# Sums of squares over four slots instead of two, a ring of 18 hidden tiles, and eight hidden units moved from GpSimd to ScalarE

## What is computed

```python
hi = x @ W1[:H];  hj = x @ W1[H:]
h = relu(hi[:, :, None, :] + hj[:, None, :, :] + b1)    # 128 x 128 pairs of nodes
y = h @ W2 + b2
y = layernorm(y) * gamma + beta                         # over the features of each pair
out = sum over j of adj[i, j] * y[i, j]
x = layernorm(x + out)
```

## Time and profile before

| what | value |
|---|---|
| median of 3 runs | 2771.56 us (2769.07 to 2772.95) |
| profiled execution | 2773.57 us, span of its instructions 2772.0 us |
| PE busy | 98% |
| PE weight loads busy | 41% |
| DVE busy | 94% |
| ACT busy | 93% |
| POOL busy | 90% |
| granted TensorE clock | 0.989 mean |

### The profile page before, as it was taken

The page is one execution under the profiler, slowest core; times in us unless marked ns, Lnnn a source line. Parts: engine busy times, 40 slices in busy tenths (PEclk is TensorE's granted clock), DMA queues, the critical chain, the costliest instruction groups (busy, mean ns, idle before and its releaser), DMA issues.

```text
span 2772.0 us, 60903 instructions
## 1 busy us (share of the span) xinstructions
PE 2707.0 (98%) x10882; PEld 1128.4 (41%) x10882; DVE 2618.7 (94%) x20102; ACT 2565.2 (93%) x6903; POOL 2491.0 (90%) x3498
## 2 busy tenths in 40 slices
PE   8999999999999999999999999999999999999993
PEld 2344444444444444444444444444444444444442
DVE  4999999999999999999999999999999999999997
ACT  7999999999999999999999999999999999999991
POOL 3899999999999999999999999999999989999992
PEclk9999999999999999999999999999999999999995
DMA  3655655655555555556556555555555565465552
GB/s 104 239 195 211 234 198 197 230 215 192 214 226 202 204 216 222 195 213 234 195 198 235 209 192 227 223 193 210 226 207 195 205 234 203 192 228 222 193 214 108
DMA packets 188668, 571.72 MB, mean 206 GB/s; under 512 B 70656, under 2 KB 106368, under 8 KB 139136
## 3 DMA queue, kind: packets, MB, share of 16 engines
q1 hardware_dynamic: 188288, 567.83, 54.5%
HBM read 555.17 MB, written 8.39 MB: 203 GB/s over the span
## 4 chain that ended last, share of the span: by engine, by line
PE 59%; DVE 13%; ACT 11%; DMA 10%; issue 5%; SPq 2%; POOL 0%; DVEq 0%; POOLq 0%; ACTq 0%
PE y_ps L416 41%; PE ss_ps L428 11%; DVE h L684 8%; ACT h L555 6%; DMA cb<-c_scratch 6%; ACT sq L565 3%; DMA c_scratch<-c 2%; DMA devs<-dev_rows 2%; SPq L324 1%; ACT dev_rows L572 1%; PE prod_bank L478 1%; PE prod_bank L482 1%; DVE h L668 1%; DVE stats L708 1%; DVE gT L684 1%
## 5 line engine op out<-in xcount | busy, mean ns | idle before, releaser
L923 POOL TENSOR_SCALAR h<-vT,uT 128x128 f32<-128x128 f32 x2520 | 2063.8, 834 | 54.1 <-ACT vT L545 44.6
L684 DVE CUSTOM_DVE_ANT_0 h<-h,cb 128x128 f32<-128x128 f32 x8192 | 2005.8, 291 | 74.4 <-DMA cb<-c_scratch 71.4
L416 PE MATMUL y_ps<-h,w2c 128*128 128x512 f32 x4096 | 2032.8, 613 | 11.9 <-DVE h L668 2.8
L555 ACT ACTIVATE h<-uv_ps,uT 128x128 f32<-128x128 f32 x4785 | 1426.9, 441 | 0.0
L565 ACT ACTIVATE sq<-y_ps,b2c_col 128x1024 f32<-128x1024 f32 x1024 | 1193.5, 1166 | 139.3 <-PE y_ps L416 138.6
L416 PEld LDWEIGHTS y_ps<-h,w2c 128*128 128x128 f32 x4096 | 672.9, 190 | 944.1 <-issue 647.3
L684 DVE DVE_READ_ACCUMULATOR2_ANT gT<- 128x1 f32 x8192 | 637.5, 78 | 0.0
L428 PE MATMUL ss_ps<-sq,sel 128*32 128x512 f32 x4096 | 545.5, 605 | 0.8 <-ACT sq L565 0.8
L914 POOL TENSOR_TENSOR rs<-var_eps,minus_half 128x1 f32<-128x1 f32 x448 | 297.9, 665 | 35.1
L911 POOL TENSOR_TENSOR var_eps<-mv,eps_col 128x1 f32<-128x1 f32 x448 | 94.8, 212 | 132.7 <-DVE mv L711 129.2
L668 DVE TENSOR_SCALAR h<-vT,uT 128x128 f32<-128x128 f32 x757 | 202.1, 295 | 4.7 <-ACT mask_all L610 2.6
(11 more groups left out here) (100 smaller groups left out, 1460.6 us busy)
## 6 DMA issues: line engine op xcount, KB each, us to landing
cb<-c_scratch SPq DMA_DIRECT2D x384, 1024.0 KB, 9.4
cb<-c_scratch SPq DMA_DIRECT2D x256, 512.0 KB, 4.9
adj_c<-in_adj_dram SPq DMA_DIRECT2D x512, 8.0 KB
devs<-dev_rows SPq DMA_DIRECT2D x512, 8.0 KB
x_in<-in_x_dram SPq DMA_DIRECT2D x64, 64.0 KB, 10.9
c_scratch<-c SPq DMA_DIRECT2D x128, 32.0 KB, 1.5
adj_in<-in_adj_dram SPq DMA_DIRECT2D x64, 64.0 KB, 4.4
x_res<-in_x_dram SPq DMA_DIRECT2D x64, 64.0 KB, 5.3
```

Source lines behind the costliest of these rows:

```text
L416: op = pe.matmul(y_ps[:, t % 2, c0:c0 + COLS], w2c[:], h[:, t, c0:c0 + COLS], start=True, stop=True)
L555: op = act.activation(h[:, t, n * P:(n + 1) * P], v, ACT.Relu, bias=uT[:, b, i:i + 1])
L684: op = dve.tensor_tensor_reduce(h[:, t, cols], h[:, t, cols], cb[:, t // 2, c0:c0 + P], 1.0, 0.0, ALU.mult, ALU.add, gT[:, i:i + 1])
L923: op = pool.tensor_scalar(h[:, t, n * P:(n + 1) * P], vT[:, b, :], uT[:, b, i:i + 1], 0.0, ALU.add, ALU.max)
```

## The change

- A group of sums now covers four slots: 16 records of L428 (L431 in the changed kernel) once in four passes, at s = 1, 5, 9 and 13, in place of 8 records at every odd s. The squares' ring grows from 4 to 6 slots.
- POOL makes two units of every slot, 32 a graph in place of 40. ACT makes the third unit of the eight slots that had one, 85 a graph in place of 77. DVE keeps its 11.
- `h` becomes a ring of 18 slots, and the weighted sums run one slot later. The later layers' steps from `g_keep` on stand one slot later too, with `turn_x` and `keep_xT`.
- SP issues the turn of the deviations ahead of the store of the output.

```diff
-TTR_LAG = START + 14
-TAIL_LAG = START + 28
+TTR_LAG = START + 15
+H_RING = 18
 LAYERS = 3
-SQ_RING = 4
-ROOTLESS = (1, 2, 4, 6, 8, 10, 13, 15)
+SQ_RING = 6
+GROUP = 4
...
-    return 3 if (t + START) % SLOTS in ROOTLESS else 2
+    return 2
...
-    ("g_keep", 2, 4), ("l0_mm", 3, 0), ("l0_sum", 3, 5), ("ln0", 3, 6), ("x1_scaled", 4, 6),
...
+    ("g_keep", 3, 4), ("l0_mm", 4, 0), ("l0_sum", 4, 5), ("ln0", 4, 6), ("x1_scaled", 5, 6),
...
-    ("l3_agg2", 23, 0), ("l3_agg_keep2", 23, 8), ("l3_mm2", 24, 0), ("l3_sum2", 25, 1), ("l3_ln2", 25, 2),
-    ("l3_relu2", 26, 6), ("final_sum", 28, 2), ("ln3", 28, 3),
...
+    ("l3_agg2", 24, 0), ("l3_agg_keep2", 24, 8), ("l3_mm2", 25, 0), ("l3_sum2", 26, 1), ("l3_ln2", 26, 2),
+    ("l3_relu2", 27, 6), ("final_sum", 29, 2), ("ln3", 29, 3),
...
-        h = sb("h", [P, SLOTS, DUO_UNITS * P])
+        h = sb("h", [P, H_RING, DUO_UNITS * P])
...
+                if new is not None:
+                    straighten_deviations(new, 0)
                 if oldest is not None:
                     wait_apart(sp, normed["ln3"], oldest + 1)
                     wait_apart(sp, out_stored, 16 * oldest)
                     sp.dma_start(out[oldest], x4[:, 1 - buf, :]).then_inc(out_stored, 16)
                 if new is not None:
-                    straighten_deviations(new, 0)
                     store_coefficients(new, 0)
...
-                half, p = t // HALF, (t % HALF) // 2
-                wait(pe, sq_done, SLOTS * g + t + 2)
-                if p == 0:
+                half = t // HALF
+                wait(pe, sq_done, SLOTS * g + t + GROUP)
+                if t % HALF == 0:
                     wait(pe, dev_done, 2 * g + half)
-                for q in range(4):
-                    c0 = (q % 2) * COLS
-                    mm = pe.matmul(ss_ps[32 * q:32 * q + 32, :], sel[:, ROWS - 1 - p:ROWS - 1 - p + 32],
-                                   sq[:, (t + q // 2) % SQ_RING, c0:c0 + COLS],
-                                   start=(p == 0), stop=(p == ROWS - 1))
+                for d in range(GROUP):
+                    p = (t + d) % HALF // 2
+                    for block in range(2):
+                        q = 2 * (d % 2) + block
+                        mm = pe.matmul(ss_ps[32 * q:32 * q + 32, :], sel[:, ROWS - 1 - p:ROWS - 1 - p + 32],
+                                       sq[:, (SLOTS * g + t + d) % SQ_RING, block * COLS:(block + 1) * COLS],
+                                       start=(p == 0), stop=(p == ROWS - 1))
                 mm.then_inc(var_summed, 1)
...
-                    if s == 11 and after is not None:
+                    if s == 12 and after is not None:
                         turn_x(after, 1 - buf)
-                    sg, t = lagging(graphs, s, START + 3)
-                    if s % 2 == 1 and sg is not None:
+                    sg, t = lagging(graphs, s, START + 1 + GROUP)
+                    if t % GROUP == 0 and sg is not None:
                         variances(sg, t)
...
-                    wait(act, ttr_done, SLOTS * (g - 1) + t + 1)
+                    wait(act, ttr_done, SLOTS * g + t - H_RING + 1)
...
-                wait(act, var_summed, SLOTS // 2 * g + (t - SQ_RING) // 2 + 1)
...
+                wait(act, var_summed, (SLOTS * g + t - SQ_RING) // GROUP + 1)
...
-                wait(act, var_summed, SLOTS // 2 * g + HALF // 2 * (half + 1))
+                wait(act, var_summed, SLOTS // GROUP * g + HALF // GROUP * (half + 1))
...
-                    if s == 12 and after is not None:
+                    if s == 13 and after is not None:
...
-                        if k == 0 and hg is not None:
-                            for n in range(DUO_UNITS + 1 - pool_units(hg, ht), DUO_UNITS):
-                                hidden(hg, hb, ht, n)
+                        if k == 0 and hg is not None and pool_units(hg, ht) > 0:
+                            hidden(hg, hb, ht, DUO_UNITS - 1)
                         if k == EARLY_AT and eg is not None and pool_units(eg, et) > 0:
-                            hidden(eg, eb, et, DUO_UNITS - pool_units(eg, et))
+                            hidden(eg, eb, et, DUO_UNITS - 2)
```

More of the change, by code:

```diff
@@ L415, in products @@
                 c0 = block_of_duo * COLS
-                op = pe.matmul(y_ps[:, t % 2, c0:c0 + COLS], w2c[:], h[:, t, c0:c0 + COLS], start=True, stop=True)
+                op = pe.matmul(y_ps[:, t % 2, c0:c0 + COLS], w2c[:], h[:, (SLOTS * g + t) % H_RING, c0:c0 + COLS], start=True, stop=True)
                 if block_of_duo == 1:
@@ L554, in hidden @@
                 v = v_ps if t < SLOTS - 1 else vT[:, b, :]
-                op = act.activation(h[:, t, n * P:(n + 1) * P], v, ACT.Relu, bias=uT[:, b, i:i + 1])
+                op = act.activation(h[:, (SLOTS * g + t) % H_RING, n * P:(n + 1) * P], v, ACT.Relu, bias=uT[:, b, i:i + 1])
                 if n == BLOCK_UNITS - 1:
@@ L563, in squares @@
                 wait(act, y_done, SLOTS * g + t + 1)
-                wait(act, var_summed, SLOTS // 2 * g + (t - SQ_RING) // 2 + 1)
-                act.activation(sq[:, t % SQ_RING, :], y_ps[:, t % 2, :], ACT.Square,
+                wait(act, var_summed, (SLOTS * g + t - SQ_RING) // GROUP + 1)
+                act.activation(sq[:, (SLOTS * g + t) % SQ_RING, :], y_ps[:, t % 2, :], ACT.Square,
                                bias=b2c_col[:], scale=float(P) ** -0.5).then_inc(sq_done, 1)
             def deviations(g, half):
-                wait(act, var_summed, SLOTS // 2 * g + HALF // 2 * (half + 1))
+                wait(act, var_summed, SLOTS // GROUP * g + HALF // GROUP * (half + 1))
                 wait(act, devs_in[half], 64 * g)
@@ L662, in hidden @@
                 if n == 0:
-                    wait(dve, ttr_done, SLOTS * (g - 1) + t + 1)
+                    wait(dve, ttr_done, SLOTS * g + t - H_RING + 1)
                     if t <= 1:
@@ L667, in hidden @@
                 i = unit_of(t, n)
-                op = dve.tensor_scalar(h[:, t, n * P:(n + 1) * P], vT[:, b, :], uT[:, b, i:i + 1], 0.0, ALU.add, ALU.max)
+                op = dve.tensor_scalar(h[:, (SLOTS * g + t) % H_RING, n * P:(n + 1) * P], vT[:, b, :], uT[:, b, i:i + 1], 0.0, ALU.add, ALU.max)
                 if n == vector_units(g, t) - 1:
@@ L683, in weighted_sum @@
                 c0 = (t % 2) * DUO_UNITS * P + n * P
-                op = dve.tensor_tensor_reduce(h[:, t, cols], h[:, t, cols], cb[:, t // 2, c0:c0 + P],
+                op = dve.tensor_tensor_reduce(h[:, (SLOTS * g + t) % H_RING, cols], h[:, (SLOTS * g + t) % H_RING, cols], cb[:, t // 2, c0:c0 + P],
                                               1.0, 0.0, ALU.mult, ALU.add, gT[:, i:i + 1])
@@ L917, in hidden @@
             def hidden(g, b, t, n):
-                wait(pool, ttr_done, SLOTS * (g - 1) + t + 1)
+                wait(pool, ttr_done, SLOTS * g + t - H_RING + 1)
                 if t == 0:
@@ L922, in hidden @@
                 i = unit_of(t, n)
-                op = pool.tensor_scalar(h[:, t, n * P:(n + 1) * P], vT[:, b, :], uT[:, b, i:i + 1], 0.0, ALU.add, ALU.max)
+                op = pool.tensor_scalar(h[:, (SLOTS * g + t) % H_RING, n * P:(n + 1) * P], vT[:, b, :], uT[:, b, i:i + 1], 0.0, ALU.add, ALU.max)
                 if n == DUO_UNITS - 1:
```

## The result

| | before | after |
|---|---|---|
| median | 2771.64 us (2769.07 to 2772.95, 4 runs) | 2887.13 us (2886.57 to 2887.52, 4 runs) |
| profiled span | 2772.0 us | 2885.3 us |

The ratio is 1.0418, with an interval of 1.04 to 1.0436: 115.5 us slower. The range held it (2830 to 2920), and the forecast of 2900 us was 13 us too high.

A forecast was written before the change was run, and what follows sets the result against it. The bound was taken to be laps of ACT and PE around the sums, not an engine's total. Period 40.7 + 3.3 = 44.05 us, +2.0 times 63 is 126, plus 2 to 3 at the end: 2771.56 + 129 = 2900 us, range 2830 to 2920.

The forecast's parts named there:

- The period: Repeating stretch of the kernel, 63 times: 40.7 us of ACT's work plus 3.3 of waits, 44.05 against 42.05 us.
- The group: PE's sums over four slots: four rounds of 0.45 plus 0.09, so 1.90 us; bounds 1.81 to 2.00.
- The lap: Two passes of ACT's units, PE's products and ACT's square around the sums; at s = 9 6.20 us, ACT waiting 1.29.
- A: Start of the ACT square that opens a lap; the other times in the lap are counted from it.
- The wait at s = 6: Deviation on ACT waiting for the sums of s = 5, possible at A + 3.92, due at A + 2.25 + 1.00: 0.67 us.
- ACT's own work: ACT's squares, units, deviations, relus, copies and other steps in a period: 38.7 us before, 40.7 with eight more units.
- POOL's units: Eight units fewer on POOL: worth nothing, as neither ACT's waits nor the lap show a wait for POOL.
- Rings and lags: Ring of 18, later sums and larger squares' ring: worth nothing per period, at most 2.5 us added at the end.
- PE's saving buys nothing: Four groups fewer save PE 1.1 us a period, but PE then waits at block 0 for ACT's fourth unit.
- PE as the bound that is freed: Rival: PE sets the period and the change relieves it, period 41.0 us, time 2706 us; chance 0.08.
- Only part of the waits comes: Rival: deviations' waits at s = 5 and 13 vanish, 2.3 us left, period 43.0, 2834 us; chance 0.12.
- The group saves nothing inside: Rival: the group takes 2.00 us or more, three laps grow by 0.10, period 44.35, 2919 us; chance 0.04.

The follow-up runs named there:

- g2_p40_lags: Kernel before with only the ring of 18, later sums and later layers' steps, and SP's order (groups of two, POOL 40): 2756.09 us, ratio 0.9949.
- g2_p32_old: Kernel before with only the eight units moved from POOL to ACT (groups of two, old ring and lags): 2810.42 us, ratio 1.0144.
- room to run ahead: Products and all behind the hidden units one slot later; with the l2 and l3 steps later too and POOL at 32 units: 2789.29 us, at 40 units 2725.36 us.
- g4_p40_ahead_l2: g4_p40_ahead_mm with the steps l2_agg to l3_relu0 one slot later as well: 2725.36 us, ratio 0.9846.
- their twin: g4_p40_ahead_l2 with groups of two slots in place of four and a squares' ring of 4: 2752.25 us, ratio 0.994.
- seven kernels with the extra slot: Kernels in which everything behind the hidden units runs one slot later, so products use units made two passes before: 2725.36 to 2789.29 us.
- g4_p40_ahead: g4_p40 with everything behind the hidden units one slot later, so products use units made two passes before: 2759.70 us, ratio 0.996.
- g4_p40_ahead_mm: g4_p40_ahead with the matmuls l3_mm1 and l3_mm2 moved from the pass's start to behind block 1: 2750.55 us, ratio 0.9925.
- g4_act88: Changed kernel with three more units moved from POOL to ACT, in passes s = 2, 9 and 10: 2887.70 us, ratio 1.042.
- g4_p40: Changed kernel with POOL's eight third units given back (POOL 40, ACT 77), groups of four kept: 2864.98 us, ratio 1.034.

## Why the prediction was right, and by how much its steps were off

**The period.** 44.05 forecast, 43.95 measured (the rounded terms, 40.7 + 3.3, give 44.0; unrounded they give 44.07). **The group** was put at 1.90 and takes 1.86. **The lap** of s = 9 was put at 6.20 and takes 6.22; block 0 started at A - 0.35, not A - 0.40.

| ACT waits, by steps | s = 2 | s = 3 | s = 6 | s = 10 | s = 14 | sum |
|---|---|---|---|---|---|---|
| forecast | 0.82 | 0.17 | 0.67 | 1.29 | 0.37 | 3.3 |
| measured | 0.85 | 0.17 | 0.54 | 1.33 | 0.47 | 3.36 |

(By the pass in which ACT stands; the working named most of them by the pass of the sums, s = 1, 5, 9 and 13, which is the one before.) The wait at s = 6 was put too long in part by a slip: by the terms as they stand (A - 0.40 + 0.96 + 0.33 + 0.86 + 0.09) that group starts at A + 1.84 and not A + 1.88, so the wait is 0.63. It measured 0.54, since the group is shorter and PE got there a little earlier (A + 1.78).

The 0.1 by which the period was too long, some 6 us of the total, lies in what was taken for ACT's own work. The step behind L539, the transpose's copy in s = 12, takes 0.16 here and not the 0.31 of the same step in the earlier trace rows. That 0.31 was a copy of 0.16 and a wait of 0.15 for PE, too short for the views of waits to name: before, the square at 1293.83 starts 0.20 after PE's last product, which ends where the next matmul starts:

```profile
1291.81 1.98 PE L416 MATMUL y_ps<-h,w2c 128*128 128x512 f32 x4
1293.63 0.38 PE L478 MATMUL prod_bank<-adj_in,x 128*128 128x128 f32 x2
```

**The terms that were priced at nothing.** POOL's units: right, its share fell to 73%, and from 300 to 2460 us the waits for POOL are none before and 0.2 us after. SP's order: nothing seen, and not tried alone. **Rings and lags, "worth nothing"**: this is the step that was wrong. Made alone with SP's order (g2_p40_lags), they take 0.5% off the time. The periods of before are not all 42.05. 11 of 59 are longer, by 0.2 to 1.5 us, and their mean is 42.18; in after all are 43.95. Multiplied by 63, a plain period took those along as if they were still there: about 7 us too many. g2_p40_lags has one such period and no `cb` wait, but g2_p32_old has one too and still 46.0 us of that wait, with a period long enough for DVE. So slack for DVE seems to take them away, whether it comes from the lags or from a longer period; then the step's own words ("the period grows") named a gain that it did not count. Which wait made the periods long before was not isolated. By parts: the last 60 periods are longer by 1.773 us on average, which gives 106.4. The first three steps add 5.1 and the end 2.1, and the start takes off 0.2. That is 113.3, the whole difference between the spans.

**The total was right, its shares mislead.** The sum said: waits unchanged, ACT's own work 2.0 more, so the units are the price. That is the bookkeeping of one kernel against another, not what each edit costs. Made alone, the units cost 0.70 a period with groups of two, 0.35 with groups of four, and 1.18 with room to run ahead; the group alone costs 1.74 with POOL at 40. Each fills or opens waits that the other made, so the prices do not add in another order. The forecast had the mechanism for it ("PE that then waits, at block 0, for ACT's fourth unit") and the longer laps, but "PE's saving buys nothing" was too kind to the group: made alone, its held-up squares and deviations cost 1.7 us a period. That the waits of ACT came out "as much as today" was so for the two edits together and for neither by itself.

**The rivals.** PE as the bound that is freed is wrong for this kernel and half right for another: from g4_p40_ahead_l2, where no product waits for a unit of the pass before, the same groups save 27 us against their twin. The Trainium skill (Perfetto Trace Analysis, Identifying the Most-Contended Engine) warns against reading matmul busy share as the engine's limit; here PE showed 98% busy in a kernel (g2_p40_lags) in which an edit that takes 1.1 us or more a period off PE made the time 109 us longer. "Only part of the waits comes" fell with the deviations' two waits, 0.54 and 0.47. "The group saves nothing inside" fell with the group's 1.86 us.

**What the misses of the study share.** All seven kernels with the extra slot came out at or above the upper end of what was expected. g4_p40_ahead and g4_p40_ahead_mm were forecast as if, with one wait gone, the path were nearly clear, and each met another step with a lag of one pass. The rule was applied to the hidden units and not to the later layers' steps.

## What to carry to other kernels

Where two engines hand work round, price a change by the lap between two hand-overs, with every item that stands in line on either side, and not by the engines' totals: work moved into a lap's wait is free (g4_act88), and an edit that takes work off an engine but bunches the rest into one lap can cost (g4_p40). Before a burst is made longer on an engine, count how many passes of look-ahead its inputs and outputs have; if there is one, lengthen the look-ahead first, for every step with that lag: here the same burst then gained 27 us where it had cost 109. And check that a kernel's periods are all alike before one of them is multiplied.

## What was not expected of the hardware

A group of 16 records of the sums takes 1.86 us, 0.05 less than the 0.09 + 4 x 0.455 that a group of 8 gives: the added two rounds take 0.43 each, the same as half a product. The other surprise is how exactly the laps hold: 0.75 us a period of added ACT instructions moved the period by less than 0.01 us.
